# Step 14 of a transformer turn: the query unit's first product placed ahead of the softmax reciprocal, its square behind it

## The reference, cut to what matters

```python
for i in range(6):
    x = attn_layer(shift_tokens(x), Wqkv[i], q_scale[i], k_scale[i], Wo[i]) + x
    x = ffn_layer(shift_tokens(x), ln_g[i], ln_b[i], W1[i], b1[i], W2[i], b2[i]) + x

def attn_layer(x, Wqkv, qs, ksc, Wo):          # 16 heads of 64, windows of 32 tokens
    q, k, v = split(x @ Wqkv, 3)
    q = q / max(norm(q), 1e-12) * qs           # per head
    k = k / max(norm(k), 1e-12) * ksc
    q = q * cos * scale + rotate_half(q) * sin * scale
    k = k * cos / scale + rotate_half(k) * sin / scale
    sim = 8 * q @ k.T, masked to this window and the one before
    return softmax(sim) @ v @ Wo

def ffn_layer(x, g, bln, W1, b1, W2, b2):
    a, gate = split(layernorm(x, g, bln) @ W1 + b1, 2)
    return a * gelu(gate) @ W2 + b2
```

## Time and profile before

| | us |
|---|---|
| median of 3 runs | 6322.74 (6322.53 to 6328.97) |
| the profiled execution | 6319.79 |
| its span, first to last instruction | 6318.0 |
| the part with turns, about | 2000 to 6245 |

### The profile page before, as it was taken

How to read it: one execution, slowest core, us unless ns; L and a number is a source line. 1 busy time by engine, 2 the same in 40 slices (tenths; PEclk the granted TensorE clock), 3 DMA queues, 4 the chain that set the end, 5 groups by cost and what they waited for, 6 DMA issues and landing times. The chain is left out here.

```text
span 6318.0 us, 104346 instructions
## 1 busy us (share of the span) xinstructions
PE 5501.6 (87%) x31072; PEld 3041.0 (48%) x31072; DVE 4225.5 (67%) x6918; ACT 3753.1 (59%) x11805; POOL 2595.8 (41%) x2014
## 2 busy tenths in 40 slices
PE   6888887777769999899989999899998999899997
PEld 3333332222325555555555555555555555555553
DVE  5677665333347777777777777767777777777775
ACT  3444443223227766667766777667666677667775
POOL 1122111000015555555555555555555555555553
PEclk9999998767779999999999999999999999999998
DMA  1000000000012222222222222222222222222222
GB/s 40 0 0 0 0 0 21 0 0 0 0 61 50 48 50 53 51 52 48 48 54 55 48 47 49 55 51 48 49 53 51 52 48 48 54 55 48 48 48 67
DMA packets 160228, 244.68 MB, mean 39 GB/s; under 512 B 51280, under 2 KB 51280, under 8 KB 158928
## 3 DMA queue, kind: packets, MB, share of 16 engines
q1 hardware_dynamic: 159696, 238.34, 15.4%
HBM read 30.52 MB, written 6.29 MB: 6 GB/s over the span
## 5 line engine op out<-in xcount | busy, mean ns | idle before, releaser
L323 POOL TENSOR_TENSOR c_Pb<-c_Pb,c_rs 96x512 f32<-96x512 f32 (+1 forms) x960 | 997.2, 1039 | 1454.9 <-DVE c_rs L715 1454.9
L385 ACT ACTIVATE c_Pb<-c_S,c_nb 96x128 f32<-96x128 f32 (+1 forms) x3840 | 1344.2, 358 | 160.8 <-DVE c_nb L706 159.5
L722 DVE COPY c_PTs<-c_S 128x384 f32<-128x384 f32 (+1 forms) x960 | 558.1, 581 | 619.7 <-PE c_S L506 618.8
L706 DVE TENSOR_REDUCE c_nb<-c_S 96x4 f32<-96x512 f32 (+1 forms) x960 | 657.3, 685 | 397.1 <-PE c_S L496 396.8
L335 POOL TENSOR_TENSOR c_rot<-c_tAB 128x1024 f32<-128x1024 f32 x384 | 910.7, 2372 | 0.8 <-DVE c_tAB L685 0.8
L396 ACT ACTIVATE c_OT<-c_PO 128x192 f32<-128x192 f32 (+1 forms) x960 | 323.6, 337 | 768.0 <-PE c_PO L520 767.5
L385 ACT ACTIVATION_READ_ACCUMULATOR c_Pb<-c_S,c_nb 96x1 f32 (+1 forms) x3840 | 756.3, 197 | 0.0
L329 POOL TENSOR_TENSOR c_sqs<-c_sq 128x512 f32<-128x512 f32 x384 | 487.8, 1270 | 608.4 <-ACT c_sq L363 608.4
L496 PE MATMUL c_S<-c_QK 64*96 64x128 f32 (+1 forms) x7680 | 664.7, 292 | 0.0
L506 PEld LDWEIGHTS c_S<-c,c_Pb 96*128 96x128 f32 (+1 forms) x3840 | 432.9, 142 | 370.3 <-issue 213.8
L520 PE MATMUL c_PO<-c_PTs,c_V 128*64 128x96 f32 (+1 forms) x7680 | 554.8, 266 | 20.1 <-issue 19.3
(11 more groups left out here) (267 smaller groups left out, 10849.6 us busy)
## 6 DMA issues: line engine op xcount, KB each, us to landing
c_QK<-c_F SPq DMA_DIRECT2D x3072, 64.0 KB, 2.0
c_stage<-in_w_heads SPq DMA_DIRECT2D x36, 256.0 KB, 2.8
a_W<-in_w_level SPq DMA_DIRECT2D x1, 3335.5 KB, 11.2
c_WT<-in_w_tails SPq DMA_DIRECT2D x6, 537.5 KB, 5.6
b_W<-in_w_level SPq DMA_DIRECT2D x1, 3133.0 KB, 10.0
c_WT<-in_w_tails SPq DMA_DIRECT2D x6, 512.0 KB, 4.0
x<-in_x SPq DMA_DIRECT2D x1, 2048.0 KB, 7.5
x_kept<-x SPq DMA_DIRECT2D x1, 2048.0 KB, 6.3
```

What stands on the lines that cost most here:

```text
L323: nc.gpsimd.tensor_tensor(p, p, r, ALU.mult).then_inc(*p_ready.up())
L385: e = nc.scalar.activation(Pb[0:m, n % 3, i, :], S[0:m, 2 * (n % 2) + r, c * SPAN_K:(c + 1) * SPAN_K], ACT.Exp, bias=nb[0:m, n % 2, i:i + ...
L706: nc.vector.tensor_reduce(nb[0:m, n % 2].rearrange("p (b c) -> p b c", b=2), S[0:m, b:b + 2, 0:2 * SPAN_K].rearrange("p b (c k) -> p b c k ...
L722: nc.vector.tensor_copy(PTs[:, n % 2].rearrange("p (b c) q -> p b c q", b=2)[:, :, :, 0:m], S[:, b:b + 2, 2 * SPAN_K:].rearrange("p b (c q ...
```

## The change

It touches three engines, in steps 12 and 13 only, and only the query unit that is projected in step 12.

- DVE: `products(jq, 0, tq)` of step 13 goes ahead of `inv_sum(12)`. It now waits for `projected` (PE's matmuls) and no longer for `squared` of its half.
- ACT: `square(jq, 0, tq)` at the end of step 12 waits for `prods` of its half (DVE's product) where it waited for `projected`. So the two read the bank in the opposite order.
- PE: `v_proj(0, 0, PA)` of step 13 waits for `squared` of half 0 as well as for `prods` of half 0.

No instruction of computation is added or removed, and no DMA.

```diff
--- before.py
+++ after.py
@@ -354,10 +354,10 @@
 
             @block.scalar
             def _(act):
-                def square(j, half, turn):
+                def square(j, half, turn, behind=False):
                     kind = j % 2
                     bank = (B_BANK if half else A_BANK)[kind]
-                    act.wait_ge(*projected.nth(2 * j + half + 1, turn))
+                    act.wait_ge(*(prods if behind else projected).nth(2 * j + half + 1, turn))
                     if not half and (j or not turn.first):
                         act.wait_ge(*added.nth(j, turn))
                     nc.scalar.activation(sq[:, half], bank[:, :], ACT.Square).then_inc(*squared.up())
@@ -443,7 +443,7 @@
                     if t == 1 and tk:
                         inverse_norm(jk, tk)
                     if t == 2 and tq:
-                        square(jq, 0, tq)
+                        square(jq, 0, tq, behind=n == 12)
                     if n == 8 and now:
                         v_copy(1, 2, PA, now)
                     if n == 13 and nxt:
@@ -661,6 +661,8 @@
                         if n == 13 and new is not None:
                             pe.wait_ge(*split.nth(2 * SPLIT_V[0] + 2, Turn(new, 0, 1)))
                         pe.wait_ge(*prods.nth(2 * jq + 1, tq))
+                        if n == 13:
+                            pe.wait_ge(*squared.nth(2 * jq + 1, tq))
                         v_proj(0, {13: 0, 18: 3}[n], PA, nxt)
 
                 pe.wait_ge(*split.nth(12, Turn(0, 0, 1)))
@@ -676,10 +678,10 @@
                     dve.wait_ge(*shifted.nth(1, turn))
                     nc.vector.tensor_tensor(xl[:, x], src, xh[:, x].bitcast(F32), ALU.subtract).then_inc(*shifted.up())
 
-                def products(j, half, turn):
+                def products(j, half, turn, free=False):
                     kind = j % 2
                     bank, table = (B_BANK[kind], TB[:, kind]) if half else (A_BANK[kind], TA[:, kind])
-                    dve.wait_ge(*squared.nth(2 * j + half + 1, turn))
+                    dve.wait_ge(*(projected if free else squared).nth(2 * j + half + 1, turn))
                     if j or not turn.first:
                         dve.wait_ge(*rotated.nth(j, turn))
                     nc.vector.tensor_tensor(tAB[:, half], bank[:, :].unsqueeze(1).broadcast_to([P, 2, SEQ]), table, ALU.mult).then_inc(*prods.up())
@@ -782,6 +784,8 @@
                         pt_copy(m2, t2)
                     if prev and n in (13, 14, 15):
                         hidden(n - 13, prev)
+                    if n == 13 and tq:
+                        products(jq, 0, tq, free=True)
                     if t1:
                         inv_sum(m1, t1)
 
@@ -801,7 +805,7 @@
                         v_copy(1, 4, PA, now)
                     if n == 17 and nxt:
                         v_copy(0, 2, PA, nxt)
-                    if t == 3 and tq:
+                    if t == 3 and tq and n != 13:
                         products(jq, 0, tq)
                     if now:
                         row_max(n, now)
```

## The result

The changed kernel takes 6252.1 us (median of 4 runs, 6247.2 to 6254.1) against 6322.6 before: a ratio of 0.9886, interval 0.9874 to 0.9898. Two later comparisons gave 0.9887 and 0.9889. That is 1.1% faster, 70.6 us, where 60.6 were forecast; 6252 lies inside the forecast 6250 to 6280, near its lower end, outside the likeliest case's own 6254 to 6269. The profiled execution took 6254.1 us, its span is 6252.3.

What follows compares the result with a forecast made beforehand. PE sets the pace as long as it is fed, and its idle time is lost. Stall 52.5 - 2.2 - 0.7 = 49.6, plus clock 11, gives 60.6 us: 6259.2 profiled, 6262 median, range 6250 to 6280.

Steps and rivals of the forecast that it cites:

- likeliest case: Whole kernel: the stall mostly goes and clock time comes back, 6262 us, own range 6254 to 6269, chance 0.66.
- The chain in step 13: DVE, ACT, PE in step 13: product fits DVE's idle time, second product 1.25 us earlier, 0.21 of PE's stall stays.
- Nothing later gave it back: Rest of the turn: whole 1.25 us kept in 42 turns, 52.5 us; rival given back or nothing, 6308 to 6323, 0.09.
- The cover of the square: ACT, step 12's end: product done 0.86 us before ACT reaches the square; rival that the square takes over, 6348, 0.05.
- The clock: PE behind step 13: less idle time keeps 2.4 GHz, 11 us back; rival without it, 6269 to 6278, 0.20.
- 0.95 each: Turns with a low clock stretch behind step 13: each such stretch costs 0.95 us, from two turns taking 180.3.
- I count 11 back: Low clock stretches behind step 13: 11 us of 12.4 regained, all but one or two of the stretches.
- Ends: 0, and 12.4: Bounds of the clock gain behind step 13: no us back, or all 12.4 us of 13 ordinary turns.
- Loss 0.55 each, 2.2 for four: Step 13 in four turns making new tables: DVE is late, second product 0.55 us later each, 2.2 us in all.

Runs made afterwards that it cites:

- the two halves: Two runs on the kernel before: only DVE's order changed (`order_alone`), 6331.1 us; only the waits changed (`waits_alone`), 6362.7 us.
- `one_ahead`: Changed kernel with one more DVE operation of about 0.6 us ahead of the product of half 0 in step 13: 6250.1 us, ratio 0.9884.
- `two_ahead`: Changed kernel with two more DVE operations, 1.2 us, ahead of the product of half 0 in step 13: 6278.2 us, ratio 0.9927.
- `old_filled`: Kernel before, with eight more matmuls, their result unread, in PE's step 13 stall, turns with new tables left out: 6305.2 us, ratio 0.9971.
- `waits_alone`: Kernel before with all the waits of the change, but the product still behind the reciprocal in DVE's queue: 6362.7 us, ratio 1.0060.
- `order_alone`: Kernel before with only the product put ahead of the reciprocal in DVE's queue in step 13, waits as before: 6331.1 us, ratio 1.0011.
- `tables_filled`: `tables_old_2`'s kernel with 16 and 14 more matmuls in PE's two long waits for DVE, in turns with new tables: 6230.9 us, ratio 0.9863.
- `tables_old_2`: Changed kernel with the old order and waits in the five turns with new tables, run a second time: 6248.7 us, ratio 0.9890.
- `filled_new_order`: `tables_filled` with the new order in the turns with new tables too: 6240.6 us, ratio 0.9867.

## Why the prediction was right, and where its size was off

**The chain in step 13** was right within 0.1 us: gain of the second product 1.26 (forecast 1.25), stall left 0.30 (0.21), DVE's wait 1.04 (about 1.0), turns 87.9 and 87.4 (87.95 and 87.4). That it needs both the order and the waits is shown by the two halves.

**Nothing later gave it back**: the whole turn shortened by what the step did. The cover of the square is as computed (`one_ahead`, `two_ahead`). In the turns with tables the loss within the step is as computed too, 0.6 us against 0.55, but only about 0.15 of it reaches the end of the turn.

**The clock.** That the 1.2 GHz stretches came from this stall was argued from rows 6 and 7; `old_filled` shows it, and `waits_alone` shows it from the other side. The Trainium skill's rule, which names long idle gaps of PE as what brings the clock down ("TensorE: Matmul & The Clock Gate", section "HAM oscillation — how this bites in real kernels"), would have given no clock term. This case's traces differ from it, and they decide: a stall of 1.47 us was followed by low stretches, and 0.59 was not. That 0.95 each was the right price is in part luck: the pair it was taken from has one turn of each kind, 0.5 and 1.4.

**The mis-sized term** is "I count 11 back" with its "Ends: 0, and 12.4". It counted only the low stretches behind step 13. The two profiled executions, from the first table load to the last, stand at 4267.5 and 4197.0 us, 70.5 less. Of this the 25 turns in the loop away from a layer's start give 42.0 (forecast: 25 x 1.25 and eleven times 0.95, 41.7) and the six of the last layer 7.9 (7.5). But the 15 turns around a layer's start give 24.7. The forecast had 13.5 there: eleven times 1.25 (the ten beside the turns with tables, and the one of those five in which the stall was seen), less 2.2 for the other four, and two low stretches back. The last turn of all lost 4.2, with a longer low clock in it. Here are the rows that sum the 15 turns (five stretches of three; sum and busy times), before and after:

```profile
sum 1443.80, PE 1292.75 PEld 775.02 DVE 1067.18 ACT 950.80 POOL 741.55; mean PE 258.55 PEld 155.00 DVE 213.44 ACT 190.16 POOL 148.31
```

```profile
sum 1419.10, PE 1282.77 PEld 769.93 DVE 1065.47 ACT 948.41 POOL 739.54; mean PE 256.55 PEld 153.99 DVE 213.09 ACT 189.68 POOL 147.91
```

DVE and ACT are busy for the same time within 3 us, PE 10 us less with the same instructions. The time at 1.2 GHz in these turns fell from 102 to 79 us by the trace. In `order_alone` it was 137 us, and the 15 turns took 1456.3. `tables_filled` shows what low clock is worth there: with 55 us of it the same turns take 1407.1, against 1424.9 and 96 us in `tables_old_2`, so 0.43 us for each microsecond at 1.2 GHz. (`filled_new_order`, with 79 us and 1417.6, gives the same.) For the 23 us that went, that is an estimate of 10 us; 2 of them stand in the 13.5 already, so 8 of the 11 missing are found. Another 1.5 or so are the term "Loss 0.55 each, 2.2 for four", which measured about 0.15 each. The last 1.5 are open.

Within the turns with tables, that low stretches follow PE's long waits for DVE is shown: filled, they keep 17 us at 1.2 GHz of 58 with the old order, and 20 of 51 with the new. In the ten turns beside them nothing of the kind is shown. That the change made the low time less because its shorter turns fall otherwise against the clock is inferred. Three profiles of the changed kernel agree (79, 79 and 75 us), of the kernel before there is one.

## What to carry to other kernels

When an engine idles at the head of its queue for a value that comes late, look for what behind it needs nothing late; but follow each of its inputs to the engine that makes it, because here the order and the waits each cost time alone and gained only together. The swap pays where the displaced reader has slack behind something slow (0.9 us behind the Gelus). Where it has none, the step loses 0.5 us or more, of which the whole turn may feel less. Price a stall of PE by its length and by the clock of what follows, over the whole kernel.

## What the runs showed of the hardware that was not expected

Matmuls whose result nobody reads, put into PE's waits, made the kernel faster: 20 us of 6325 with eight in each ordinary turn, and 18 us of 6249 with thirty in each of five turns. A stall of 1.47 us was followed by a stretch at 1.2 GHz in 14 of 42 turns (18 of 41 in `order_alone`), one of 1.87 (1.78 in the last layer) in 37 of 41, and one of 0.59 or 0.30 in none of 41. Such a stretch of 3.4 us cost 0.5 us of a turn's 89 where it began about the end of the stall, and 1.3 where it began 2 us behind it.
